# The last layer's expert feed-forward on tokens sorted by expert, in tiles of 256 rows whose weights are fetched by expert number

## What is computed

```python
def _L3_ffn_ref(x, Wg, bg, W1, b1, W2, b2):      # 8 experts, hidden 512
    gate_scores = softmax(x @ Wg + bg)
    top1_idx = argmax(gate_scores)
    top1_mask = one_hot(top1_idx, 8)
    top1_weight = sum(gate_scores * top1_mask)
    h = silu(einsum('btd,edh->bteh', x, W1) + b1)
    o = einsum('bteh,ehd->bted', h, W2) + b2
    return sum(o * top1_mask) * top1_weight
...
s = _L3_attn_ref(xn, ...)        # causal, decayed, linear attention
g = _silu(_L3_ffn_ref(xn, ...))
x = x + s * g
```

## Time and profile before

| | |
|---|---|
| median of 3 runs | 1600.83 us (1599.22 to 1602.33) |
| the profiled execution's own time | 1603.26 us |
| its span, first to last instruction | 1601.4 us |
| PE busy | 1423.2 us, 89% |
| DVE busy | 1152.5 us, 72% |
| ACT busy | 695.4 us, 43% |
| POOL busy | 624.3 us, 39% |
| mean granted TensorE clock | 0.955 of full |

### The profile page before, as it was taken

One profiled execution on the slowest core, in us unless ns is written; L12 is line 12 of the kernel. 1 busy time (PEld: TensorE's weight loads), 2 busy tenths in 40 slices (PEclk: granted clock), 3 DMA queues, 4 the chain that ended last, 5 costly groups with the idle time before them and its releaser, 6 DMA issues.

```text
span 1601.4 us, 14629 instructions
## 1 busy us (share of the span) xinstructions
PE 1423.2 (89%) x4802; PEld 496.3 (31%) x4802; DVE 1152.5 (72%) x1700; ACT 695.4 (43%) x963; POOL 624.3 (39%) x297
## 2 busy tenths in 40 slices
PE   5999998898999977799987999989989778899998
PEld 2444333111211111112122343333333223344443
DVE  7777554888888899988834965777878988754333
ACT  3434333555565554556551323232334434353443
POOL 0233435677767764477770002243242442200000
PEclk8999999999999999999998999999999889999999
DMA  5100200110101000300001000000011000000000
GB/s 188 35 28 24 64 20 29 38 33 25 37 22 36 26 25 25 121 17 15 21 15 48 1 0 1 0 1 0 13 40 40 26 0 1 7 1 0 7 7 7
DMA packets 40154, 41.78 MB, mean 26 GB/s; under 512 B 16528, under 2 KB 27920, under 8 KB 40080
## 3 DMA queue, kind: packets, MB, share of 16 engines
q1 hardware_dynamic: 31664, 40.50, 7.9%
q10 hardware_dynamic: 8416, 0.36, 0.3%
HBM read 32.39 MB, written 8.00 MB: 25 GB/s over the span
## 4 chain that ended last, share of the span: by engine, by line
PE 51%; DVE 28%; POOL 7%; issue 7%; ACT 4%; DMA 1%; ACTq 0%; SPq 0%; DVEq 0%; POOLq 0%
PE ps L100 50%; POOL psum_sb L106 7%; DVE small L119 6%; DVE ar L106 6%; DVE small L106 5%; ACT ar L137 3%; DVE ar L119 2%; DVE on_sb L106 2%; DVE ps_sb L106 1%; DVE osb L119 1%; PE ps L103 1%; ACT L137 1%; DVE acc_sb L106 1%; DVE ar L114 1%; DVE psum_sb L106 1%
## 5 line engine op out<-in xcount | busy, mean ns | idle before, releaser
L100 PE MATMUL ps<-ar 64*128 64x512 bf16 (+5 forms) x2992 | 881.8, 548 | 62.4 <-DVE ar L106 28.2
L137 ACT ACTIVATE ar<-ps 128x1024 f32<-128x1024 f32 (+1 forms) x352 | 317.8, 907 | 344.7 <-PE ps L100 310.9
L100 PEld LDWEIGHTS ps<-ar 64*128 64x128 bf16 (+4 forms) x2992 | 262.9, 141 | 609.5 <-issue 470.2
L119 DVE TENSOR_REDUCE small<-ps 128x2 f32<-128x1024 f32 (+1 forms) x272 | 310.4, 1157 | 50.7 <-PE ps L100 49.3
L106 POOL TENSOR_TENSOR psum_sb<-psum_sb,ar 128x1024 f32<-128x1024 f32 x128 | 309.7, 2419 | 68.7 <-ACT ar L137 56.2
L106 POOL TENSOR_TENSOR ar<-ar 128x2048 f32<-128x2048 f32 (+1 forms) x32 | 139.5, 4372 | 387.6 <-ACT ar L134 300.0
L100 PE MATMUL ps<-xnT,ar 128*128 128x512 f32 x528 | 275.5, 624 | 3.5 <-DVE ar L106 3.5
L106 DVE TENSOR_TENSOR ar<-ar 128x512 f32<-128x512 f32 (+1 forms) x188 | 167.2, 898 | 121.4 <-ACT ar L137 112.6
L137 ACT ACTIVATE ar<-ps,wA 128x512 f32<-128x512 f32 x128 | 87.7, 687 | 154.4 <-PE ps L100 139.8
L100 PEld LDWEIGHTS ps<-xnT,ar 128*128 128x128 f32 x528 | 97.8, 196 | 108.8 <-issue 103.1
L106 DVE TENSOR_TENSOR ar<-ar,ps 128x512 f32<-128x512 f32 (+1 forms) x104 | 70.6, 680 | 75.1 <-PE ps L100 68.0
(11 more groups left out here) (118 smaller groups left out, 1089.4 us busy)
## 6 DMA issues: line engine op xcount, KB each, us to landing
rec_sb<-lscr SPq DMA_DIRECT2D x64, 128.0 KB, 2.9
scr<-ar SPq DMA_DIRECT2D x48, 128.0 KB, 1.9
ar<-in_L_w SPq DMA_DIRECT2D x8, 544.0 KB, 7.0
ar<-in_L_w SPq DMA_DIRECT2D x8, 512.0 KB, 3.5
ar<-scr SPq DMA_DIRECT2D x32, 112.0 KB
ar<-in_L_w SPq DMA_DIRECT2D x12, 256.0 KB, 7.5
ar<-scr SPq DMA_DIRECT2D x32, 96.0 KB
xs<-in_x SPq DMA_DIRECT2D x4, 256.0 KB, 6.6
```

The source lines that it names most:

```text
L100: return self.e.matmul(o, l, r, start=start, stop=stop) if self.e else Nothing()
L119: return self.e.tensor_reduce(o, a, AX.X, op, negate=True) if negate else self.e.tensor_reduce(o, a, AX.X, op)
L137: return self.e.activation(o, a, fn, **kw) if self.e else Nothing()
```

## The change

The feed-forward of layer 3 leaves the block scheme. The 128 blocks, gates(3, c) and bias(3) are gone. For each batch h (two chunks, 1024 tokens) there is now:

- **route3(h)**, 6 slots, right after ln(3, 2h + 1): scores of the 8 sub-blocks of 128 tokens, softmax and first maximum as before but for the whole batch; then the rank of each token in its expert (a scan on DVE and three small bf16 matmuls with a triangle and with ones), the first slot of each expert rounded up to tiles of 256, the slot number of each token (slot3) and the expert number of each of the 11 tiles (eu3). POOL scatters the 1024 normed rows to DRAM (x3s) with 8 indirect DMAs of 128 rows. SP loads weights of the first three tiles (dma_of reads the number from SBUF into a register, then one DMA of 128 x 1156 floats: W1, W2, b1 and b2 of that expert), waits for the scatters, and loads the first three tiles of rows.
- **moe3(h)**, the main generator from slot START3[h] = 107 and 155: 11 tiles, two slots each and two more. Per tile: 2 transposes of the rows, an ACT copy, 4 matmuls of 256 columns with W1, 4 silus of 256 columns with bias, 4 matmuls with W2, a DVE copy, 2 transposes back, a DVE add of b2, a store to DRAM (y3s). Loads run three tiles ahead, five weight buffers in turn.
- **gather3(h)**, one slot, at 131 and 179: POOL waits for the last stores and gathers the 1024 result rows with 8 indirect DMAs into gT; ACT takes silu(gate * row), eight times 128 columns.
- **end3(c)** transposes s first and multiplies and adds with tokens on partitions.

The number of tiles is fixed: 11 always run, filled or not. x3s is first filled with the input x by six DMAs at the start (DRAM to DRAM). Slots between 96 and 107, 131 and 155 have no main step. att3 starts at 113, 121, 133 and 141; ln(3, 2) waits for the first batch's scatters, whose source buffer it reuses.

```diff
-    [(0, "tables"), (0, "rec", 0), (0, "rec", 1), (0, "bias", 2), (0, "bias", 3), (0, "position"),
-     (30, "rec", 2), (54, "rec", 3), (104, "l3start")] + [((113, 113, 126, 154)[c], "att3", c) for c in range(NC)],
+    [(0, "tables"), (0, "rec", 0), (0, "rec", 1), (0, "bias", 2), (0, "position"),
+     (30, "rec", 2), (54, "rec", 3), (104, "l3start")] + [((113, 121, 133, 141)[c], "att3", c) for c in range(NC)],
...
-    [((61, 85, 109, 133)[c], s, *a) for c in range(NC) for s, *a in (("end2", c), ("ln", 3, c), ("gates", 3, c))],
-    [(130 + 32 * c, "end3", c) for c in range(NC)],
+    [((61, 85, 109, 133)[c], s, *a) for c in range(NC)
+     for s, *a in (("end2", c), ("ln", 3, c)) + ((("route3", c // 2),) if c % 2 else ())],
+    [(max(START3[h] + 2 * NT3 + 2, first), s, *a) for h in range(2)
+     for first, s, *a in ((0, "gather3", h), (0, "end3", 2 * h), (138, "end3", 2 * h + 1))],
...
+            xtr(0)
+            for j in range(NT3 + 1):
+                if j >= 2:
+                    ytr(j - 2)
+                if j + 1 < NT3:
+                    xtr(j + 1)
+                if j < NT3:
+                    up(j, 0)
+                    up(j, 1)
+                    yield
+                    up(j, 2)
+                    up(j, 3)
+                if j >= 1:
+                    down3(j - 1)
+                yield
+            ytr(NT3 - 1)
...
+        def gather3(h):
+            for k in range(2):
+                pool.wait_ge(*at(f"y3_out{k}", NT3 * h + NT3 - 1 - (NT3 * h + NT3 - 1 - k) % 2))
+            for i in range(8):
+                pool.wait_ge(*at("gated", 2, 2 * h + i // 4))
+                pool.gather(gT[:, 128 * (8 * h + i):128 * (8 * h + i) + 128], y3s[h], slot3[h][:, i:i + 1]).then_inc(
+                    *landed((f"rows3_in{i}", h, i)))
...
+        def gather3(h):
+            for i in range(8):
+                c = 2 * h + i // 4
+                g = gT[:, 128 * (8 * h + i):128 * (8 * h + i) + 128]
+                act.wait_ge(*at(f"rows3_in{i}", h, i))
+                act.wait_ge(*at("route_dve", h, "gate"))
+                act.af(g, g, ACT.Silu, scale=gate3[h][:, i:i + 1]).then_inc(
+                    *(up(("g3_act",), ("g3", c)) if i % 4 == 3 else up(("g3_act",))))
...
+            for j in range(NT3 + 1):
+                if j >= 2:
+                    store(j - 2)
+                if j + 3 < NT3:
+                    load_w3(h, j + 3)
+                    load_x3(h, j + 3)
```

More of the change, by code:

```diff
@@ L57 @@
 STEPS = {"ln": 6, "gates0": 5, "qk": 7, "v": 2, "max0": 20, "end0": 3, "gates": 7, "tables": 14, "rec": 5,
-         "bias": 1, "position": 3, "end1": 2, "ffn2": 9, "tile": 12, "end2": 2, "l3start": 2, "att3": 12, "end3": 3,
-         "tail0": 4}
+         "bias": 1, "position": 3, "end1": 2, "ffn2": 9, "tile": 12, "end2": 2, "l3start": 2, "att3": (8, 12, 8, 12), "end3": 3,
+         "route3": 6, "gather3": 1, "tail0": 4}
+TILE = 256
+NT3 = (1024 + NE * (TILE - 1)) // TILE
+NW = 5
+START3 = (107, 155)
 LANES_A = [
@@ L140, in dma, with scatter, gather, dma_of @@
         return self.e.dma_start(o, i) if self.e else Nothing()
+    def scatter(self, rows, index, i):
+        if not self.e:
+            return Nothing()
+        return self.e.indirect_dma_start(rows, bass.IndirectOffsetOnAxis(ap=index, axis=0), i, None)
+    def gather(self, o, rows, index):
+        if not self.e:
+            return Nothing()
+        return self.e.indirect_dma_start(o, None, rows, bass.IndirectOffsetOnAxis(ap=index, axis=0))
+    def dma_of(self, o, table, nc, index):
+        if not self.e:
+            return Nothing()
+        e8 = nc.values_load(index, engines=[mybir.EngineType.SP], min_val=0, max_val=NE - 1,
+                            skip_runtime_bounds_check_because="the number is held to the last expert where it is made")
+        return self.e.dma_start(o, table[bass.ds(e8, 1), :, :].rearrange("a p k -> (a p) k"))
 class Marks:
@@ L206, in lane_steps @@
             yield
-        part = stages[name](*args) if name in stages else iter(())
-        for _ in range(STEPS[name]):
+        part = (stages[name](*args) if name in stages else None) or iter(())
+        n = STEPS[name]
+        for _ in range(n if isinstance(n, int) else n[args[0]]):
             next(part, None)
@@ L256, in _program @@
     identb = cb[:, 0:128]
+    below, onesb = (cb[:, CB_N - 256 + 128 * i:CB_N - 128 + 128 * i] for i in range(2))
     def area(off, n):
@@ L797, in down @@
             pe.wait_ge(*at("hidden", n))
[L798 to L803, removed]
+            ins = pe.mm(ps[:, 4, :], down_weights(n), h_buf[n % 4][0:width(n), :], start=first, stop=end)
             ins.then_inc(*(filled(4, ("ffn", layer, c), ("down", n)) if end else up(("down", n))))
@@ L1411, in ffn13 @@
                 yield
+            yield from ffn_rest(moe3)
         stages = {"ln": ln, "gates0": gates0, "gates": gates, "qk": qk, "v": v, "max0": max0, "tail0": tail0,
                   "end0": end0, "end1": end1, "end2": end2, "tables": tables, "rec": rec, "position": position,
-                  "ffn2": ffn2, "tile": tile, "att3": att3, "end3": end3, "bias": bias, "l3start": l3start}
+                  "ffn2": ffn2, "tile": tile, "att3": att3, "end3": end3, "route3": route3, "bias": bias, "l3start": l3start}
         weave(ffn0(), LANES_A, stages)
@@ L1659, in scalar_program @@
         stages = {"ln": ln, "gates0": gates0, "gates": gates, "qk": qk, "max0": max0, "tail0": tail0,
-                  "ffn2": ffn2, "tile": tile, "att3": att3, "l3start": l3start}
+                  "ffn2": ffn2, "tile": tile, "att3": att3, "l3start": l3start, "route3": route3, "gather3": gather3}
         weave(ffn0(), LANES_A, stages)
@@ L1738, in ffn13 @@
                 yield
+            yield from ffn_rest(lambda h: range(2 * NT3 + 2))
         weave(ffn0(), LANES_A, {})
         weave(attention(), LANES_B, {})
-        weave(ffn13(), LANES_C, {"tile": tile})
+        weave(ffn13(), LANES_C, {"tile": tile, "route3": route3, "gather3": gather3})
     def sync_program(sp):
@@ new lines, in load_x3, with route3 @@
+        def load_x3(h, j):
+            J = NT3 * h + j
+            sp.wait_ge(*at("x3T", J - 3) if J >= 3 else at("down", len(blocks) - 1))
+            sp.dma(v3(xin3[J % 3], 128), x3s[h][TILE * j:TILE * j + TILE, :].rearrange("(k p) d -> p k d", p=128)).then_inc(
+                *landed((f"x3_in{J % 3}", J)))
+        def route3(h):
+            for _ in range(5):
+                yield
+            sp.wait_ge(*at("route_dve", h, "experts"))
+            for j in range(3):
+                load_w3(h, j)
+            sp.wait_ge(*at("sorted3", h))
+            for j in range(3):
+                load_x3(h, j)
@@ L1896, in ffn13 @@
+        def ffn13():
+            for _ in blocks:
                 yield
-        stages = {"qk": qk, "max0": max0, "tail0": tail0, "l3start": l3start, "end3": end3}
+            yield from ffn_rest(moe3)
+        stages = {"qk": qk, "max0": max0, "tail0": tail0, "l3start": l3start, "end3": end3, "route3": route3}
         weave(ffn0(), LANES_A, stages)
```

366 lines of the change are left out of this document (278 added, 88 removed).

## The result

The change makes the kernel faster: 1503.66 us median of 4 runs (1502.17 to 1506.95) against 1600.96 before, ratio 0.9396, 95% interval 0.9376 to 0.9415. The forecast was 1500, in a range of 1470 to 1560. The total came out; some terms inside it did not, and the experiments look for the reasons.

The account below looks back on a forecast made before the run. DVE was taken to bound slots 96 to 131, PE the rest. Slot-by-slot terms, with 53.3 us of batch 1 tiles, a 17.9 tail and +6 clock, gave 1500.2, plus 1.9, minus 2.4: 1500 us, range 1470 to 1560.

Parts of the forecast that it names:

- The matmuls saved in PE's stretch: After 1397 us, where PE is the bound, saved matmuls count in full; batch 1's tiles 4.84 us each.
- rival D: PE's clock stays at half in batch 1's tiles: +44 us, 1544 us in all; chance 0.06.
- rival E: Tiles wait for their weights, 7.0 us a tile: +24 us, 1524 us in all; chance 0.06.
- The bare chain: Uncovered dependent steps: last store to ln 24.5 us, routing 13, scatter and load 13.3, tail 17.9.
- rivals B and F: Dearer indirect DMAs: B 2.9 us each, 1536 in all, chance 0.15; F 6.1, slower than before, 0.04.
- The prediction's 1517: Estimate if the twenty indirect DMAs on the path did not overlap at all, 43 us in place of 22.
- Slots 96 to 107: Twelve slots taking 49.0 us before: 8.3 off for DVE multiplications, 4 on for route3(0), ending at 1283.
- The +4: Slots 96 to 107: 4 us added for route3(0)'s eight indirect DMAs between POOL's two pairs of products.
- The -8.3: Slots 96 to 107: twelve multiplications of 0.69 us leave DVE, 8.3 us off.
- Rival C: Attention pairs shrink more, DVE less held by POOL: slots 96 to 131 shorter by 22, 1478; chance 0.12.
- Slots 108 to 131: Took 103.9 us; priced by DVE's savings and additions at 87.5, so slot 132 begins at 1370.5, not 1393.5.
- The clock term: From slot 131 to the first tile PE runs partly at half clock: +6 us, between 0 and 12.

Follow-up runs that it names:

- e2: Changed kernel with each tile's transposes back moved in PE's stream behind the first two W1 products two tiles later; 1490.89 us, 0.9297 of before.
- e8: Changed kernel with batch 1's eight gathers issued twice, first into a free buffer; 1512.81 us, 0.9431 of before.
- e4: Changed kernel with three of the four W2 products left out in batch 0's tiles; 1488.88 us, 0.9300 of before.
- e5: Changed kernel with two more DVE reductions of 128 x 512 in every tile of batch 0; 1511.21 us, 0.9432 of before.
- e9: Changed kernel with mixer stages att3(1) to att3(3) started four slots later, at 125, 137 and 145; 1483.21 us, 0.9277 of before.
- e11: Changed kernel with 16 unread bf16 matmuls of 512 columns in PE's stream at slot 132; 1499.75 us, 0.9376 of before.

## Why the prediction was right, and where it was not

**The matmuls saved in PE's stretch are worth their time: right.** Of the 100.6 us of span, 98.9 were won behind the pair of slot 97, and the tiles of batch 1 take 53.3 us where 55.0 were forecast (4.69 a tile; the clock 0.97, against rival D's 0.50; loads landed in 4.1 and 3.8 us three tiles ahead, against rival E). e2 showed the 0.8 us of idle a tile that the sum had named. (The 848 KB of DMA a tile in the sum should be 834: 578 of weights, 128 of rows in and 128 out. Nothing hung on it.)

**The bare chain: right to within 1.5 us in each part.** Store, gathers, end2 and ln were put at 24.5 us; from the last tile's add, some 2 us before the first gather, to the end of ln(3, 3)'s copy they take about 24. Forecast and measured are 13 and 14.5 for routing, 13.3 and 14.5 for scatter and load, 17.9 and 18.8 for the tail. The indirect DMA at 1.26 in place of 1.1 explains 1.3 us of each batch of eight; rivals B and F needed 2.9 and 6.1, and e8 confirms 1.25. The Trainium skill, "DMA: Bandwidth & Descriptors", section on the anatomy of one DMA by the gpsimd path, gives about 2.0 us plus bytes / 436e3, an estimate of 2.15 us for such a DMA. That is near the 2.5 us to landing, while the next one starts after 1.26, so DMAs issued one after another overlap in part. The prediction's 1517 for the case without overlap is a slip: its own terms, 43 in place of 22, give 1521.

**Slots 96 to 107: direction right, size too small.** -4.3 was forecast, -10.5 came (51.3 to 40.8). The +4 charged for the scatter on POOL is the term that failed: the eight DMAs fit into POOL's idle gap, and its second products start 20.9 us after the first, against 20.8 before. The -8.3 came nearly whole, as DVE's busy time there fell from 44.6 to 37.2 us. The rest is idle time of DVE, 3.6 us in place of 6.7; what ended it the traces do not show in full, and in runs with the stretch's second value the whole is 8.6 to 8.9. Rival C did not come. DVE still stands still during POOL's products, only in fewer and other operations:

```profile
1261.75 9.76 DVE L116 TENSOR_TENSOR ar<-ar 128x512 f32<-128x512 f32 x2
...
1412.49 0.17 DVE L138 TENSOR_TENSOR_SCAN rt<-rt 128x8 f32<-128x8 f32 x1
```

The first row is two operations of 0.69 us that fell on the second products. The second is a scan of route3(1), with nothing on POOL; the same scan of route3(0), at 1241.42 beside the first products, took 3.71 us.

**Slots 108 to 131: wrong.** The step "So 87.5, and slot 132 begins at 1370.5" took 16.4 us off; from the pair of slot 109 on, the kernel before needs 94.5 us (53.0 + 41.5) to block 131, and the kernel after 97.0 (54.9 + 42.1) to the first gather and some 95 to its last tile. Two things failed in it. It priced DVE alone, by "PE's load hardly changes", when PE was busy 46.3 of 53.0 us in half of that stretch: with DVE's share cut, PE and the hand-overs carry on as before (e4, e5). And it left the move of att3(1) by four slots unpriced; e9 shows that this is 8.1 us of the third stretch. So the forecast was wrong by halves: with att3(1) where it stood, the third stretch takes 34.0 us against 41.5 before, near half of what the sum took off both (part of it may be clock, 0.88 before and 1.00 in e9), while the second takes 54.9 against 53.0, none at all. In e9 the first gather comes 129.7 us after the pair of slot 97; from the 1240.6 of the kernel after, that is 1370.3.

**The clock term.** +6 was added on top of the links. It is there: e11 finds 3.1 us in the routing stretch, e9 up to 8.0 in three stretches (with the moved work in them). But the links' measured times contain it: 52.6 us from the last tile of batch 0 to the first product of batch 1, against 50.8 + 6 forecast. The Trainium skill, "TensorE: Matmul & The Clock Gate", part 1, says that activity lifts half clock; e11 agrees, 0.76 to 1.00 by fillers.

**Why the total was right all the same.** In the trace the last tile of batch 0 ends near 1376 (its add, 128x256, at 1375.9), 5.6 us after the 1370.5 of the sum: some 11 lost from the pair of slot 109 on and 0.9 before that of slot 97, 6.2 won between the two. From there to the first product of batch 1 the kernel took 4.2 us less than forecast, in the tiles 1.7 less, in the tail 0.9 more. 5.6 - 4.2 - 1.7 + 0.9 is 0.6 us. That the number fell so close is luck of signs. Had slots 96 to 107 given only what was forecast, the kernel would have taken 1510; without the clock term, which the measured links already contain, the forecast would have been 1494. The range holds both.

Left open is how much of e9's 4.2 and 0.8 us behind slot 141 is clock and how much the later att3(2) and att3(3). No run separates them.

## What to carry to other kernels

When a change replaces dense work by a chain of dependent steps, price the chain step by step: here 146 us of matmuls were saved and 97 returned, with some 70 us of gather, norm, routing, scatter and tail standing bare. In streams that run in order, independent work belongs in the gaps of such a chain, not in the busy stretch before it: moving three mixer stages by four slots was worth more (16.1 us by the distances) than either single edit to the sorted part (10.2 and 8.9). And a stretch where two engines are both over 80% busy need not shrink when one of them is relieved: with DVE cut from 45.6 to 33.1 us the one from slot 109 to 121 took 54.9 us in place of 53.0.

## What the runs showed of the hardware

Idle time of PE was paid twice here: behind a stall in which PE was busy 14.7 of 21.3 us, the same routing instructions took 14.5 us at a mean granted clock of 0.76, between its levels of 1.2 and 2.4 GHz, instead of 11.4 at 1.00 (2.4 GHz), and 16 matmuls of no use in the stall brought it back (e11). While POOL works on its products DVE can stand still: a scan of 8 columns took 3.71 us beside them and 0.17 without. An indirect DMA of 128 rows takes 0.95 us of POOL as a gather (mean of 16) and 1.03 and 0.99 as a scatter (two groups of 8, by source buffer), some 1.26 from one to the next; I had bounded it between 0.37 and 2.9. A weight fetch by a number that DVE had just written went out 0.5 us after it (the number at 1414.65, the first load's issue at 1415.12), so the register read cost little.
